# Two attentions over 257 keys: maxima by bank, one product for the last keys of four batches, heads added ahead of the output projection

## The chip, the cores and the metric

One core of one Trainium2 chip runs the whole program. The metric is the device time of one execution in microseconds, the median of several runs. The engines are TensorE (PE in the rows; PEld is its weight load), VectorE (DVE), ScalarE (ACT), GpSimd (POOL) and SyncE (SP, which here issues DMAs). Each engine works through its own list of instructions in order, and they meet at semaphores.

## The reference

A perceiver of four layers on x (128 batches, 32 tokens, 128 features) with a context of 257 keys for each batch. Each layer has a cross-attention, a self-attention (or a scan) and a feed-forward part. The change lies in the cross-attentions of layers 1 and 2. Cut to what matters (the norms of q and k in layer 1 and the mask of layer 2 are left out; 16 heads of 8 features):

```
q = x1 @ Wq.T ; k = ctx @ Wk.T ; v = ctx @ Wv.T      # split into 16 heads
s = einsum('bhqd,bhkd->bhqk', q, k) * scale          # 32 x 257 for each batch and head
a = softmax(s, axis=-1)
o = einsum('bhqk,bhkd->bhqd', a, v)                  # heads side by side: 32 x 128
x = x + o @ Wo.T + bo
```

## The kernel before

`cross_attention` is called twice: in stage l1x_att (keys already projected and stored in KA, fetched by DMA into kT) and in stage l2x_att (KA is None: the keys are projected here, and there is a mask). It handles one batch at a time. The 16 heads are four groups j of four: the group j lies on partitions 32j to 32j + 31, and within it each of the 128 rows of the score product is one (head of four, query) pair. So a batch has four score products of 128 x 257, one in each of the four banks of pS. In float32 a product is issued as two passes, so the rows show x8 for four products, x4 for two.

The keys 0 to 255 and the last key 256 are handled apart. For the first 256: maxima over pS (`maxima`, DVE, L2666: two reduces, of two banks each), exponentials with their sums (`exponentials`, ACT, L2626, one for each bank, into prob), reciprocals (`factors`, DVE, L2671), scaling (`scale`, POOL, L2427), eight turns of 128 x 128 (`turn`, PE, L2546, into the banks pT), copies of them (`keep_turned`: half by DVE, L2688, half by ACT, L2633, into probT), and `attend` (PE, L2559), which gives O: feature by (head of four, query). `own_head` (DVE, L2698 or L2695) multiplies O with the mask m4, so that for each feature only its own head of the four is left, and stores it in own[:, h, b, :], b being the batch's place in a group of four. `output` (PE, L2566) then runs once for four batches: X = sum over h of own[:, h] @ wo, four products, and to the same X it adds the last keys' part.

The last key: its probabilities of four batches are gathered in tail (POOL, L2433) and turned on PE (`turn_tails`, L2508) to 16 rows (batch, j); `keep_tails` (DVE, L2681) multiplies them with batch16 into pbd, so that a row counts for its own batch alone. Its values, masked by head (vm, POOL, L2438), are multiplied with wo in four products (`last_keys`, PE, L2514, two in each of two slots), which ACT copies to mt (L2618). `output` multiplies pbd with mt, four products with 16 rows (L2570), into X. DVE adds X to the residual (`add`, L2704); POOL adds the bias bo.

The order is written by hand. `run_slots4` calls `slot(n, c, k)` on each engine, with c = n % 4 and k = n // 4: in slot n, PE makes the scores of batch n + 1, attends for n - 2, turns n - 1 and makes the values of n + 2 (and in l2x_att its keys, ahead of the turns). Work that belongs to four batches stands in slots chosen by c. The slots with 4 <= n < 124 are a loop over four slots; below, a slot is named by its c. The bank pKV holds in turn the keys' projection (columns 0 to 256), the values (0 to 255), and at its end the last keys' products and the turned tails (columns 256 to 511), so `bank_read` and `bank_free` make PE wait until it has been read: in l2x_att for k_kept, DVE's copy kT (L2676). `after(eng, sem, n)` waits until unit n is through; s_made is counted twice for each batch.

In this excerpt of PE's slot, the lines that the order turns on:

```python
if c == 0 and inside(n - 4):
    turn_tails(k - 1)
...
if c == 0 and inside(n - 4):
    pe.wait_ge(pb_made, made(k - 1))
...
if c == 3 and inside(n):
    last_keys(k, 0)
if c == 0 and inside(n - 4):
    last_keys(k - 1, 1)
...
if c == 1 and inside(n - 5):
    output(k - 1)
```

`cosine_attention` (stage l3a_att) is another function; its POOL instruction at L1867 waits for s_made as well.

## Time and profile before

| | us |
|---|---|
| median of 3 runs | 4020.48 |
| lowest, highest | 4013.39, 4028.0 |
| span of the profiled execution | 4018.7 |

The page gives the profiled execution's span (from the first to the last instruction) and no time of its own beside it.

| engine | busy, whole span | busy, l1x_att 900 to 1300 us | busy, l2x_att 1980 to 2420 us |
|---|---|---|---|
| PE | 3136.4 (78%) | 361.96 of 400 | 420.93 of 440 |
| DVE | 2425.2 (60%) | 251.13 | 289.26 |
| ACT | 2065.1 (51%) | 287.05 | 284.75 |
| POOL | 1963.5 (49%) | 251.94 | 246.82 |

The scores of l1x_att begin at 827.0 us and its last operations are at 1342.7; those of l2x_att at 1905.4 and 2482.1. An execution is read from the profile like this: a timeline row gives the start, how long a run of like instructions took, the engine, the line, what is written and read, and in brackets how long the engine had sat idle and who ended that. The start of the same line's next run gives the slot.

### The profile page before, as it was taken

The numbers are of one execution on the slowest core, as the hardware profiler recorded it, in microseconds if no ns is written. First come the engines' busy times: TensorE is split into PE (matmuls) and PEld (weight loads), VectorE is DVE, ScalarE is ACT, GpSimd is POOL, SyncE is SP. The second block draws the span as 40 slices with busy tenths as digits, with TensorE's granted clock in tenths as the row PEclk, the third lists the DMA queues.
The fourth block names the chain that finished last, engine by engine and source line by source line (L and its number), as shares of the span: only waits on it lengthen the run. The fifth ranks groups of instructions, "written<-read, shape, count | busy, mean of one in ns | idle before, by whom it ended". The sixth has DMA issues, their size and how long they took to land. (4 is left out here: it accounts for less than half of the span.)

```text
span 4018.7 us, 81101 instructions
## 1 busy us (share of the span) xinstructions
PE 3136.4 (78%) x24323; PEld 2160.5 (54%) x24323; DVE 2425.2 (60%) x5893; ACT 2065.1 (51%) x6409; POOL 1963.5 (49%) x1960
## 2 busy tenths in 40 slices
...
DMA packets 138613, 233.70 MB, mean 58 GB/s; under 512 B 28428, under 2 KB 100398, under 8 KB 137623
## 3 DMA queue, kind: packets, MB, share of 16 engines
...
q8 instruction: 103, 1.69, 0.2%
...
## 5 line engine op out<-in xcount | busy, mean ns | idle before, releaser
L2427 POOL TENSOR_TENSOR l2x_att_prob<-l2x_att_prob,l2x_att_rs 128x1024 f32<-128x1024 f32 x128 | 242.2, 1893 | 253.2 <-DVE l2x_att_rs L2671 253.2
L3200 PE MATMUL l2a_pY<-l2a_hc,ident 128*128 128x512 f32 x512 | 275.0, 677 | 90.3 <-POOL l2a_hc L3119 56.1
L2427 POOL TENSOR_TENSOR l1x_att_prob<-l1x_att_prob,l1x_att_rs 128x1024 f32<-128x1024 f32 x128 | 242.2, 1893 | 190.6 <-DVE l1x_att_rs L2671 190.6
L2626 ACT ACTIVATE l2x_att_prob<-l2x_att_pS,l2x_att_nmx 128x257 f32<-128x257 f32 x512 | 236.2, 474 | 169.4 <-DVE l2x_att_nmx L2666 169.4
L3089 POOL TENSOR_TENSOR l2a_dbu<-l2a_dx,l2a_BC 128x1024 f32<-128x1024 f32 x128 | 298.5, 2352 | 21.5 <-PE l2a_pY L3200 10.7
L2626 ACT ACTIVATE l1x_att_prob<-l1x_att_pS,l1x_att_nmx 128x257 f32<-128x257 f32 x512 | 236.2, 474 | 129.7 <-DVE l1x_att_nmx L2666 129.7
L3217 ACT ACTIVATE l2a_pA<-l2a_dl,l2a_A 128x512 f32<-128x512 f32 x256 | 174.4, 689 | 188.8 <-DVE l2a_pH L3323 113.0
L3200 PEld LDWEIGHTS l2a_pY<-l2a_hc,ident 128*128 128x128 f32 x512 | 103.7, 211 | 253.2 <-issue 120.0
L3323 DVE TENSOR_TENSOR_SCAN l2a_pH<-l2a_pA,l2a_dbu 128x512 f32<-128x512 f32 x192 | 224.8, 1216 | 23.6 <-POOL l2a_dbu L3089 12.2
L2666 DVE TENSOR_REDUCE l2x_att_nmx<-l2x_att_pS 128x2 f32<-128x514 f32 x256 | 165.5, 688 | 115.7 <-PE l2x_att_pS L2534 113.0
L2666 DVE TENSOR_REDUCE l1x_att_nmx<-l1x_att_pS 128x2 f32<-128x514 f32 x256 | 165.5, 689 | 92.4 <-PE l1x_att_pS L2527 92.3
L1963 ACT ACTIVATE l3a_att_prob<-l3a_att_pS,l3a_att_nmx 128x128 f32<-128x128 f32 x512 | 179.6, 397 | 8.2 <-DVE l3a_att_nmx L2000 4.1
L1874 POOL TENSOR_TENSOR l3a_att_prob<-l3a_att_prob,l3a_att_rs 128x512 f32<-128x512 f32 x128 | 130.4, 1041 | 56.7 <-DVE l3a_att_rs L2021 56.7
L2207 POOL TENSOR_SCALAR l1x_KA<-l1x_k_y,l1x_k_cols 128x257 f32<-128x257 f32 x128 | 118.0, 940 | 53.3 <-DVE l1x_k_y L2329 53.3
L2546 PE MATMUL l1x_att_pT<-ident,l1x_att_prob 128*128 128x128 f32 x1024 | 139.0, 279 | 0.0
L2546 PE MATMUL l2x_att_pT<-ident,l2x_att_prob 128*128 128x128 f32 x1024 | 133.7, 274 | 0.0
L2546 PEld LDWEIGHTS l2x_att_pT<-ident,l2x_att_prob 128*128 128x128 f32 x1024 | 119.5, 142 | 14.2 <-issue 0.6
L2546 PEld LDWEIGHTS l1x_att_pT<-ident,l1x_att_prob 128*128 128x128 f32 x1024 | 112.0, 142 | 19.5 <-issue 13.4
...
L3330 DVE TENSOR_TENSOR l2a_hc<-l2a_pH,l2a_BC 128x512 f32<-128x512 f32 x192 | 121.7, 676 | 0.0
L1963 ACT ACTIVATION_READ_ACCUMULATOR l3a_att_prob<-l3a_att_pS,l3a_att_nmx 128x1 f32 x512 | 120.9, 236 | 0.0
L2527 PE MATMUL l1x_att_pS<-l1x_att_kT,l1x_att_qb 32*128 32x257 f32 x1024 | 96.5, 432 | 19.5 <-ACT l1x_att_prob L2626 17.6
...
## 6 DMA issues: line engine op xcount, KB each, us to landing
l2a_BC<-l2a_rows SPq DMA_DIRECT2D x128, 512.0 KB, 3.8
...
l1x_att_ctx<-ctx_t SPq DMA_DIRECT2D x128, 128.5 KB, 2.1
l1x_att_kT<-l1x_KA SPq DMA_DIRECT2D x128, 128.5 KB, 2.2
l2x_att_ctx<-ctx_t SPq DMA_DIRECT2D x128, 128.5 KB, 2.1
...
```

The costliest lines, as they stand in the source:

```text
L1874: pool.tensor_tensor(x, x, bc(rs[:, n % 2, R * j:R * j + R], 2, P), ALU.mult).then_inc(scaled, 1)
L1963: last = act.activation(prob[:, n % 3, h, :], pS[:, j, h % R * P:(h % R + 1) * P], ACT.Exp, bias=nmx[:, n % 2, h:h + 1], accum_out=sums[:, ...
L2207: pool.tensor_scalar(parts[i].dst[:, piece(n, u)], y[:, n % 3, u, 0:width(n)], cols[i][:, 0:1], None, ALU.add).then_inc(done, 1)
L2427: pool.tensor_tensor(p, p, bc(rs[:, b, :], 2, LAST), ALU.mult).then_inc(scaled, 1)
L2546: last = pe.transpose(pT[h][:, j * P:(j + 1) * P], prob[:, b, j, h * P:(h + 1) * P], env.ident[:, :])
L2626: last = act.activation(prob[:, b, j, 0:KEYS], pS[:, j, 0:KEYS], ACT.Exp, bias=nmx[:, b, j:j + 1], accum_out=sums[:, b, j:j + 1])
L2666: dve.tensor_reduce(nmx[:, b, 2 * u:2 * u + 2], pS[:, 2 * u:2 * u + 2, 0:KEYS], AX.X, ALU.max, negate=True).then_inc(m_made, 1)
L3089: pool.tensor_tensor(dbu[:, u % 3], dx[:, g % 2], bc(BC[:, u % RING, 0, :], 1, NC), ALU.mult).then_inc(dbu_made, 1)
L3200: last = pe.matmul(pY[c][:, :], env.ident[:, :], hc[:, u % 3, c, :], start=False, stop=n == NS - 1)
L3217: act.activation(pA[c][:, :], dl[:, g % 2, c, :], ACT.Exp, scale=A[:, c, n:n + 1]).then_inc(da_made, 1)
L3323: dve.tensor_tensor_scan(h, pA[c][:, :], dbu[:, u % 3, c, :], 0.0, ALU.mult, ALU.add).then_inc(h_made, 1)
L3330: dve.tensor_tensor(hc[:, u % 3, c, :], pH[c][:, :], BC[:, u % RING, 1, :], ALU.mult).then_inc(hc_dve, 1)
```

## The change

- *Maxima.* All four score products of a batch give one signal, s_made (one count for each batch; the waits on it in `queries`, SP's loads and `keys` are rewritten to that). DVE makes four reduces of 128 x 257, each with its own signal, and each exponential waits for its own bank's. PE waits for p_made once for each batch as before.
- *Last keys.* tail, vm, pbd and mt have 128 rows: row 32 h + (batch, j), 16 of 32 used in each quarter; vm and tail are cleared once by two memsets on POOL. `last_keys` is one product of 128 x 128 in c = 0 (L2520 of the new file), copied by one ACT instruction of 128 x 128. `turn_tails` is four products of 32 x 32 into the bank of O and X (the tile PT), in c = 1 behind `attend`. `keep_tails` is one instruction of 128 x 128, in c = 1 too. batch32 is loaded in place of batch16. `output` has one product for the last keys in place of four.
- *Heads.* A new DVE reduce, `sum_heads` (c = 1), adds own over h into osum (128 x 128, four elements each, 128 elements apart); `output` has one product with wo in place of four, and waits for osum_made. On DVE, pbd and the sum stand between `own_head` and, in l2x_att, `keys` (kT), and ahead of `keep_turned`. `own_head` waits for pt_made in the fourth batch of a group, and for osum_made in the first.
- *Others.* POOL adds the bias behind `queries`. In `cosine_attention`, POOL's wait ahead of kb is `n - 2` for `2 * (n - 2) + 1`, s_made being counted twice a batch there still; the names of the stages are unchanged.

The diff, cut to its core:

```diff
@@ cosine_attention, gpsimd
-                    after(pool, s_made, 2 * (n - 2) + 1)
+                    after(pool, s_made, n - 2)
@@ cross_attention
-        m16, batch16 = st.sb("m16", [P, R, R]), st.sb("batch16", [16, BT])
-        vm, tail = st.sb("vm", [P, R, 16]), st.sb("tail", [P, BT, R])
-        pbd, mt = st.sb("pbd", [16, R, BT, S]), st.sb("mt", [16, R, D])
+        m16, batch32 = st.sb("m16", [P, R, R]), st.sb("batch32", [P, BT])
+        vm, tail = st.sb("vm", [P, R, 32]), st.sb("tail", [P, 32])
+        pbd, mt = st.sb("pbd", [P, BT, S]), st.sb("mt", [P, D])
+        osum = st.sb("osum", [P, BT, S])
...
-        O, X = pO[:, 0:P], pO[:, P:2 * P]
+        O, X, PT = pO[:, 0:P], pO[:, P:2 * P], pO[:, 2 * P:2 * P + S]
+        M = pKV[:, 3 * D:4 * D]
@@ gpsimd
+                pool.memset(vm[:, :, :], 0.0).then_inc(cleared, 1)
+                pool.memset(tail[:, :], 0.0).then_inc(cleared, 1)
...
@@ tensor
-                def turn_tails(k):
-                    pe.wait_ge(tail_kept, made(2 * k + 1))
-                    pe.wait_ge(mo_kept, made(2 * k))
-                    pe.transpose(pKV[0:16, 3 * D:4 * D], tail[:, :, :].rearrange("p b j -> p (b j)"), env.ident[:, :]
-                                 ).then_inc(pt_made, 1)
+                def turn_tails():
+                    for h in range(R):
+                        r = slice(32 * h, 32 * h + 32)
+                        last = pe.matmul(PT[r, :], tail[r, :], env.ident[r, r])
+                    last.then_inc(pt_made, 1)
...
+                def last_keys(k):
                     pe.wait_ge(vm_made, made(k))
+                    after(pe, mo_kept, k - 1)
+                    pe.matmul(M, vm[:, :, :].rearrange("p h j -> p (h j)"), wo[:, :]).then_inc(mo_made, 1)
...
                 def output(g):
-                    pe.wait_ge(own_made, made(4 * g + 3))
-                    for h in range(R):
-                        pe.matmul(X, own[:, h].rearrange("p b q -> p (b q)"), wo[:, :], start=h == 0, stop=False)
-                    pe.wait_ge(mo_kept, made(2 * g + 1))
+                    pe.wait_ge(osum_made, made(g))
+                    pe.matmul(X, osum[:, :, :].rearrange("p b q -> p (b q)"), wo[:, :], start=True, stop=False)
+                    pe.wait_ge(mo_kept, made(g))
                     pe.wait_ge(pb_made, made(g))
-                    for h in range(R):
-                        last = pe.matmul(X, pbd[:, h].rearrange("p b q -> p (b q)"), mt[:, h, :], start=False,
-                                         stop=h == R - 1)
-                    last.then_inc(out_made, 1)
+                    pe.matmul(X, pbd[:, :, :].rearrange("p b q -> p (b q)"), mt[:, :], start=False, stop=True
+                              ).then_inc(out_made, 1)
...
+                    if c == 1 and inside(n - 5):
+                        pe.wait_ge(tail_kept, made(2 * (k - 1) + 1))
                     if inside(n - 2):
                         attend(n - 2, (c - 2) % 4, k if c >= 2 else k - 1)
+                    if c == 1 and inside(n - 5):
+                        turn_tails()
@@ scalar
-                def exponentials(n, b, k, u):
-                    act.wait_ge(m_made, made(2 * n + u))
+                def exponentials(n, b, k):
...
-                    for j in (2 * u, 2 * u + 1):
+                    for j in range(R):
+                        act.wait_ge(m_made, made(R * n + j))
@@ vector
-                def maxima(n, b, u):
-                    dve.wait_ge(s_made, made(2 * n + u))
-                    dve.tensor_reduce(nmx[:, b, 2 * u:2 * u + 2], pS[:, 2 * u:2 * u + 2, 0:KEYS], AX.X, ALU.max,
-                                      negate=True).then_inc(m_made, 1)
+                def maxima(n, b):
+                    dve.wait_ge(s_made, made(n))
+                    for j in range(R):
+                        dve.tensor_reduce(nmx[:, b, j:j + 1], pS[:, j, 0:KEYS], AX.X, ALU.max, negate=True
+                                          ).then_inc(m_made, 1)
...
+                def sum_heads(k):
+                    dve.wait_ge(own_made, made(4 * k + 3))
+                    after(dve, out_made, k - 1)
+                    dve.tensor_reduce(osum[:, :, :].rearrange("p b q -> p (b q)"),
+                                      own[:, :, :, :].rearrange("p h b q -> p (b q) h"), AX.X, ALU.add
+                                      ).then_inc(osum_made, 1)
```

PE in the loop of l1x_att, slot c = 0 (pS are the scores, pO attend's products, pT the turns, pKV here the last keys' products and, from L2502 or L2508 of the new file, the values; REGISTER_ALU and ISA rows belong to waits). Before:

```order
L2527 MATMUL l1x_att_pS<-l1x_att_kT,l1x_att_qb 128x257 x4
L1449 REGISTER_ALU
L2559 MATMUL l1x_att_pO<-l1x_att_probT,l1x_att_v 32x128 x8
L2506 ISA
L2507 REGISTER_ALU
L2508 MATMUL l1x_att_pKV<-ident,l1x_att_tail 16x128
L2541 REGISTER_ALU
L2546 MATMUL l1x_att_pT<-ident,l1x_att_prob 128x128 x8
L2587 REGISTER_ALU
L2497 REGISTER_ALU
L2514 MATMUL l1x_att_pKV<-l1x_att_wo,l1x_att_vm 16x128 x2
L2502 MATMUL l1x_att_pKV<-l1x_att_wv,l1x_att_ctx 128x128 x2
```

and after:

```order
L2532 MATMUL l1x_att_pS<-l1x_att_kT,l1x_att_qb 128x257 x4
L2553 REGISTER_ALU
L1449 REGISTER_ALU
L2561 MATMUL l1x_att_pO<-l1x_att_probT,l1x_att_v 32x128 x8
L2543 REGISTER_ALU
L2548 MATMUL l1x_att_pT<-ident,l1x_att_prob 128x128 x8
L2503 REGISTER_ALU
L2518 REGISTER_ALU
L2520 MATMUL l1x_att_pKV<-l1x_att_wo,l1x_att_vm 128x128
L2508 MATMUL l1x_att_pKV<-l1x_att_wv,l1x_att_ctx 128x128 x2
```

The turned tails left this slot, and one product of 128 x 128 stands where two of 16 rows stood.

PE in the same loop, slot c = 1. Before:

```order
L2527 MATMUL l1x_att_pS<-l1x_att_kT,l1x_att_qb 128x257 x4
L2559 MATMUL l1x_att_pO<-l1x_att_probT,l1x_att_v 32x128 x8
L2541 REGISTER_ALU
L2546 MATMUL l1x_att_pT<-ident,l1x_att_prob 128x128 x8
L2502 MATMUL l1x_att_pKV<-l1x_att_wv,l1x_att_ctx 128x128 x2
L2566 MATMUL l1x_att_pO<-l1x_att_wo,l1x_att_own 128x128 x4
L2570 MATMUL l1x_att_pO<-l1x_att_mt,l1x_att_pbd 128x128 x4
```

and after:

```order
L2532 MATMUL l1x_att_pS<-l1x_att_kT,l1x_att_qb 128x257 x4
L2577 ISA
L2561 MATMUL l1x_att_pO<-l1x_att_probT,l1x_att_v 32x128 x8
L2514 MATMUL l1x_att_pO<-ident,l1x_att_tail 32x32 x4
L2548 MATMUL l1x_att_pT<-ident,l1x_att_prob 128x128 x8
L2508 MATMUL l1x_att_pKV<-l1x_att_wv,l1x_att_ctx 128x128 x2
L2567 MATMUL l1x_att_pO<-l1x_att_wo,l1x_att_osum 128x128
L2570 MATMUL l1x_att_pO<-l1x_att_mt,l1x_att_pbd 128x128
```

The tails are turned here, behind attend; the output is two products for eight.

DVE in the loop of l2x_att, slot c = 1 (rs reciprocals, nmx maxima, own the masked copy, kT the keys' copy, probT the copy of the turns, pbd the last keys' probabilities, osum the sum over heads). Before:

```order
L2671 RECIPROCAL l2x_att_rs<-l2x_att_sums 128x4
L2665 ISA
L2666 TENSOR_REDUCE l2x_att_nmx<-l2x_att_pS 128x2
L2665 REGISTER_ALU
L2666 TENSOR_REDUCE l2x_att_nmx<-l2x_att_pS 128x2
L2695 SCALAR_TENSOR_TENSOR l2x_att_own<-l2x_att_pO,l2x_att_cols,m 128x4x32
L2674 REGISTER_ALU
L2676 TENSOR_SCALAR l2x_att_kT<-l2x_att_pKV,l2x_att_cols 128x257
L2686 REGISTER_ALU
L2688 COPY l2x_att_probT<-l2x_att_pT 128x512
```

and after:

```order
L2665 RECIPROCAL l2x_att_rs<-l2x_att_sums 128x4
L2660 TENSOR_REDUCE l2x_att_nmx<-l2x_att_pS 128x1 x4
L2692 REGISTER_ALU
L2694 REGISTER_ALU
L2699 SCALAR_TENSOR_TENSOR l2x_att_own<-l2x_att_pO,l2x_att_cols,m 128x4x32
L1449 REGISTER_ALU
L2676 TENSOR_TENSOR l2x_att_pbd<-l2x_att_pO,l2x_att_batch 128x128
L2682 TENSOR_REDUCE l2x_att_osum<-l2x_att_own 128x128
L2668 REGISTER_ALU
L2670 TENSOR_SCALAR l2x_att_kT<-l2x_att_pKV,l2x_att_cols 128x257
L2687 ISA
L2689 COPY l2x_att_probT<-l2x_att_pT 128x512
```

Two instructions came between own and kT, and the two reduces of the maxima are four.

## Rows read from the trace of the kernel before

**Rows 1.** Windows: from:to, length, busy us by engine, PEclk (granted clock), DMA share, GB/s

```profile
526.00:608.00 82.00, 62.64 (x155) 24.14 (x155) 72.35 (x298) 3.04 (x6) 1.69 (x2) 0.94 0.02 4
900.00:1300.00 400.00, 361.96 (x4269) 270.38 (x4271) 251.13 (x556) 287.05 (x1060) 251.94 (x303) 1.00 0.23 66
1980.00:2420.00 440.00, 420.93 (x4781) 314.63 (x4779) 289.26 (x643) 284.75 (x1041) 246.82 (x296) 1.00 0.12 30
```

**Rows 2.** Timeline of l1x_att: start us, took us, engine line, names, count [idle before]

```profile
1001.50 0.72 PE L2527 MATMUL l1x_att_pS<-l1x_att_kT,l1x_att_qb 32*128 32x257 f32 x8 [0.44 <-ACT l1x_att_prob L2626]
...
1002.25 1.29 DVE L2666 TENSOR_REDUCE l1x_att_nmx<-l1x_att_pS 128x2 f32<-128x514 f32 x2 [0.59 <-PE l1x_att_pS L2527]
...
1003.07 0.48 ACT L2626 ACTIVATE l1x_att_prob<-l1x_att_pS,l1x_att_nmx 128x257 f32<-128x257 f32 x1 [0.86 <-DVE l1x_att_nmx L2666]
...
1003.66 0.68 DVE L2688 COPY l1x_att_probT<-l1x_att_pT 128x512 f32<-128x512 f32 x1
...
1003.74 0.61 PE L2514 MATMUL l1x_att_pKV<-l1x_att_wo,l1x_att_vm 128*16 128x128 f32 x4
...
1004.79 0.21 ACT L2626 ACTIVATION_READ_ACCUMULATOR l1x_att_prob<-l1x_att_pS,l1x_att_nmx 128x1 f32 x1
...
1005.06 0.72 PE L2527 MATMUL l1x_att_pS<-l1x_att_kT,l1x_att_qb 32*128 32x257 f32 x8
...
1009.39 0.72 PE L2527 MATMUL l1x_att_pS<-l1x_att_kT,l1x_att_qb 32*128 32x257 f32 x8
...
1013.75 0.49 PE L2527 MATMUL l1x_att_pS<-l1x_att_kT,l1x_att_qb 32*128 32x257 f32 x3
...
1017.34 0.72 PE L2527 MATMUL l1x_att_pS<-l1x_att_kT,l1x_att_qb 32*128 32x257 f32 x8 [0.44 <-ACT l1x_att_prob L2626]
```

**Rows 3.** Timeline of l2x_att, one group of four slots

```profile
2203.23 0.49 PE L2527 MATMUL l2x_att_pS<-l2x_att_kT,l2x_att_qb 32*128 32x257 f32 x3
...
2206.91 0.72 PE L2527 MATMUL l2x_att_pS<-l2x_att_kT,l2x_att_qb 32*128 32x257 f32 x8
...
2209.84 0.60 PE L2514 MATMUL l2x_att_pKV<-l2x_att_wo,l2x_att_vm 128*16 128x128 f32 x4
...
2210.38 0.71 PE L2502 MATMUL l2x_att_pKV<-l2x_att_wv,l2x_att_ctx 128*128 128x128 f32 x4
...
2211.02 0.71 PE L2527 MATMUL l2x_att_pS<-l2x_att_kT,l2x_att_qb 32*128 32x257 f32 x8
...
2215.84 0.72 PE L2527 MATMUL l2x_att_pS<-l2x_att_kT,l2x_att_qb 32*128 32x257 f32 x8
...
2216.69 1.29 DVE L2666 TENSOR_REDUCE l2x_att_nmx<-l2x_att_pS 128x2 f32<-128x514 f32 x2 [1.58 <-PE l2x_att_pS L2534]
...
2218.16 0.48 DVE L2676 TENSOR_SCALAR l2x_att_kT<-l2x_att_pKV,l2x_att_cols 128x257 f32<-128x257 f32 x1
...
2218.69 0.71 PE L2502 MATMUL l2x_att_pKV<-l2x_att_wv,l2x_att_ctx 128*128 128x128 f32 x4
...
2219.24 1.06 PE L2566 MATMUL l2x_att_pO<-l2x_att_wo,l2x_att_own 128*128 128x128 f32 x8
...
2220.22 1.04 PE L2570 MATMUL l2x_att_pO<-l2x_att_mt,l2x_att_pbd 16*128 16x128 f32 x7
...
2221.00 0.49 PE L2527 MATMUL l2x_att_pS<-l2x_att_kT,l2x_att_qb 32*128 32x257 f32 x3
```

**Rows 4.** Groups by line, DVE: form xcount | busy us, mean ns | idle before

```profile
L2666 DVE TENSOR_REDUCE l1x_att_nmx<-l1x_att_pS 128x2 f32<-128x514 f32 x256 | 165.5, 689 | 92.4 <-PE l1x_att_pS L2527 92.3
...
L1761 DVE TENSOR_REDUCE l1a_att_sums<-l1a_att_prob 128x16 f32<-128x512 f32 x32 | 21.8, 680 | 2.3 <-ACT l1a_att_prob L1688 2.1
...
L3656 DVE TENSOR_REDUCE l3x_att_m<-l3x_att_pS 128x1 f32<-128x257 f32 x32 | 13.6, 425 | 14.4 <-PE l3x_att_pS L3541 14.4
...
L814 DVE TENSOR_TENSOR l1f_list_z<-l1f_list_pp,l1f_list_cum 128x256 f32<-128x256 f32 x1 | 0.6, 585 | 0.0
...
L812 DVE TENSOR_TENSOR l1f_list_cum<-l1f_list_cum,l1f_list_tot 128x256 f32<-128x256 f32 x1 | 0.4, 425 | 0.0
```

More of the change, by code:

```diff
@@ L2415, in _ @@
                 st.open(pool)
+                pool.memset(vm[:, :, :], 0.0).then_inc(cleared, 1)
+                pool.memset(tail[:, :], 0.0).then_inc(cleared, 1)
                 pool.wait_ge(loaded, 16 * len(loads))
                 pool.wait_ge(vt_kept, 1)
+                pool.wait_ge(cleared, 2)
                 def queries(n, b):
-                    after(pool, s_made, 2 * (n - 2) + 1)
+                    after(pool, s_made, n - 2)
                     pool.tensor_tensor(qb[:, b % 2], bc(QT[:, bass.ds(n * S, S)], 1, R), bc(env.m4[:, :], 2, S),
@@ L2451, in slot @@
                         queries(n + 2, c + 2)
+                    if c == 0 and inside(n):
+                        x = env.X[:, k, :]
+                        pool.tensor_tensor(x, x, bo[:, :], ALU.add).then_inc(biased, 1)
                     if c == 1 and inside(n):
@@ L2464, in slot @@
                     if KA is not None:
-                        after(sp, s_made, 2 * (n - 2) + 1)
+                        after(sp, s_made, n - 2)
                     sp.dma_start(ctx[:, c % 2, 0:KEYS], env.a.ctx_t[:, bass.ds(n * KEYS, KEYS)]
@@ L2484, in bank_read @@
                     after(pe, v_kept, n - 1)
-                    if c < 2:
-                        after(pe, mo_kept, 2 * (k - 1) + c)
+                    if c == 1:
+                        after(pe, mo_kept, k - 1)
                 def keys(n, c, k):
@@ L2523, in scores @@
                         pe.wait_ge(k_landed[b], landed_count(c, k, 1))
-                    after(pe, p_made, 2 * (n - 1) + 1)
+                    after(pe, p_made, n - 1)
                     for j in range(R):
@@ L2528, in scores @@
                                          start=True, stop=not masked)
-                        if not masked and j % 2:
-                            last.then_inc(s_made, 1)
                     if masked:
@@ L2535, in scores @@
                                              start=False, stop=True)
-                            if j % 2:
-                                last.then_inc(s_made, 1)
+                    last.then_inc(s_made, 1)
                 def turn(n, b, h):
@@ L2636, in slot @@
                     if inside(n + 1):
-                        for u in range(2):
-                            exponentials(n + 1, (c + 1) % 4, k if c < 3 else k + 1, u)
+                        exponentials(n + 1, (c + 1) % 4, k if c < 3 else k + 1)
                     if inside(n - 1):
@@ L2674, in keys @@
                     dve.wait_ge(k_made, made(n))
-                    after(dve, s_made, 2 * (n - 2) + 1)
+                    after(dve, s_made, n - 2)
                     dve.tensor_scalar(kT[:, c % 2, 0:KEYS], pKV[:, 0:KEYS], cols[:, 0:1], None, ALU.add
```

68 lines of the change are left out of this document (28 added, 40 removed).

## The prediction

> **What bounds the kernel now.** I looked first at the windows view [rows 1], then at two timelines, and last at the DVE durations. The two attention stages with 257 keys (l1x_att, some 516 us; l2x_att, some 577 us) keep TensorE busy for 362 of 400 us and 421 of 440 us, with the full clock granted (1.00) [rows 1]. The share alone doesn't say that PE's work is the bound; what repeats, slot after slot, is a ring of waits. In the timeline of l1x_att [rows 2] the reader is to follow one slot (one batch): the scores start at 1001.50; the first of two maxima 0.75 later; the first exponential 0.82 after that; the last read of its sums ends at 1005.00, 1.93 after the first exponential began; and 0.06 later the next scores start at 1005.06. That is 3.56 us, and the PE row at 1001.50 says that it waited for ACT. All four score products end together, so nothing else stands between. Two of four slots are longer: from 1005.06 to 1009.39 (4.33; c = 0, turned tails and the last keys' products) and to 1013.75 (4.36; c = 1, the output products). Four slots take 15.84 us (1001.50 to 1017.34).
> In l2x_att [rows 3] four slots take 17.77 us (2203.23 to 2221.00): 3.68 (c = 2), 4.11 (c = 3), 4.82 (c = 0), 5.16 (c = 1). Here a second ring runs through DVE: scores at 2215.84, maxima 0.85 later, kT at 2218.16 (1.47 after the maxima began) for 0.48, and 0.05 later the values products, which need the bank that kT was read from; 0.64 after values come the next scores (2210.38 to 2211.02).
>
> **The change part by part.** All of it is priced per group of four slots; each stage has 32 groups, and I count 31, since the last drains without new scores.
>
> *Maxima bank by bank.* A reduce of 128x257 from PSUM takes 425 ns in l3x_att, against 689 for the 514 wide one [rows 4]. So the first exponential comes 0.26 us earlier. Nothing is lost by waiting for all four score products. A reduce is issued some 0.08 before its predecessor ends (two of 0.689 take 1.29 in [rows 2]), so four take 4 x 0.425 - 3 x 0.085 = 1.44, which is 0.15 more on DVE. The exponentials start 0.455 apart, further than the 0.34 of the reduces, so only the first waits. Where the ring over ACT decides, a slot goes from 3.56 to 3.30. I take 3.29 (3.55 less 0.26) for c = 2, 3 and 0 of l1x_att. Can PE follow? In c = 3 the scores are followed after 2.24 by the last-key products (1003.74), these after 0.54 by values, these after 0.64 by scores [rows 2, 3]: 3.42, with them. Now they are gone from c = 3, and in c = 0 one product (two passes) stands for four passes: 2.24 + 0.32 + 0.64 = 3.20, just under 3.29. So c = 0 falls from 4.33 to 3.29; the turned tails, and PE's wait for pbd, leave that slot.
> In l2x_att the DVE ring takes over: 0.85 + (1.47 + 0.15) + 0.48 + 0.05 puts values at 3.00 and the next scores at 3.64. The ACT ring would give 3.42. So c = 2 goes from 3.68 to 3.64, c = 3 from 4.11 to 3.64, and c = 0, with one product more (0.32), from 4.82 to 3.96.
>
> *Last keys as one 128-row product.* Two passes for eight, one ACT copy of 128x128 for two of 16x256; pbd is 128x128 for 16x512. The pass costs 0.11 (eight from 2219.24 to 2220.22 [rows 3]), and four with their gap take 0.54, so two take 0.32. That is in the slots above. ACT has room: in [rows 2] it idles in each slot before the first exponential. The four 32x32 products that turn the tails stand in c = 1 behind the attend products; between 0.1 and 0.4 us, and hidden in both stages, because PE will wait there for DVE anyway. That cover is some 0.5 us in l1x_att.
> A rule of the Trainium skill speaks against them: "TensorEngine Tiling (Array Packing)", Key Properties, has a change of tiling mode drain the engine. No row prices a change to 32x32; if it were the 0.2 that other gaps show, twice a group, the cover above would still hold it.
>
> *Heads added on DVE.* The output falls from 16 passes (2219.24 to 2221.00: 1.76) to four: 0.32 + 0.42 = 0.74, the 0.42 being two passes and the 0.20 that values show ahead of scores (0.64 - 0.44). It now waits for the sum of 512 elements, which stands behind four maxima, the masked copy and pbd. A contiguous reduce of 512 takes 680 ns [rows 4]. But this one reads each element 512 bytes from the last. The nearest row is L814: a tensor_tensor whose SBUF input steps by 128 bytes takes 585 ns, where L812 of the same 256 elements takes 425 [rows 4]: 0.625 ns more for each. For 512 elements that is 0.32, so I take 1.00 us, and keep 0.68 as the lower end; the upper end is open, and I put it at 1.3.
> The Trainium skill has the same: "SBUF — State Buffer", Specifications (TRN2), says of cachelines that one needs two hits per line for full bandwidth and that "each cross to a new line pays a penalty". By that rule L814's extra is the line crossing, and the trace agrees (585 against 425); without it the sum would be 20 us lower.
> In l1x_att, c = 1: the copy of probT starts 1.41 after the first maximum [rows 2]; that place, 0.15 later, is now pbd's: 0.75 + 1.56 = 2.31. Then pbd (0.20 on the queue), the sum (1.00) and 0.05: PE goes on at 3.56, and the next scores start at 3.56 + 0.74 = 4.30. Before it was 4.36, so the slot gains almost nothing: 12 passes are paid for with a wait.
> In l2x_att, c = 1, kT is queued behind pbd and the sum: values at 3.00 + 0.20 + 0.92 = 4.12, output 0.55 later (2218.69 to 2219.24), scores 0.74 after that: 5.41. Before 5.16: this slot is longer. Queued behind the sum there are also the copy of probT and the reciprocal; both have over 0.5 us left, since PE's next scores are late too.
>
> *Free edits.* The waits of POOL and SP on s_made count one per batch for two: the same event. POOL's x + bias goes behind the queries; POOL is busy for 252 of 400 us [rows 1], so it isn't late. The two memsets run once in a stage, while loads land. The edited wait in cosine attention (l3a) is met in both forms, as POOL has waited for rs_made of the same batch: no effect.
>
> **The sum.** l1x_att: 3 x 3.29 + 4.30 = 14.17 for 15.84, saves 1.67. l2x_att: 3.64 + 3.64 + 3.96 + 5.41 = 16.65 for 17.77, saves 1.12. Together 2.79 x 31 = 86.5. The profiled execution's span is 4018.7; less 86.5 it is 3932.2. The median of the runs shown is 1.8 above that span, so I predict 3934.
>
> **Rivals.**
> *A, the strided sum costs no more than a contiguous one (0.68):* 0.32 x 62 less: 3914. For it: the other input of L814, from PSUM, steps too, and no reduce in the trace has such a step. Against it: the 160 ns.
> *B, the maxima help less.* If the reduces don't overlap, each slot of l2x_att and c = 1 of l1x_att get 0.26 more: 5 x 0.26 x 31 = 40, so 3974. If the exponentials gain nothing from the earlier first maximum, 3 x 0.26 x 31 = 24, so 3958. Against both: the pair in [rows 2] overlaps, and ACT's row names the maxima.
> *C, slower: the strided sum becomes the bound.* Each microsecond of it beyond 1.00 costs 62 us, as PE (and kT) wait for it once a group. From 2.4 us on the change loses; at four times the contiguous price (2.7) the time is 3934 + 105 = 4039. Against it: it needs 4.7 ns an element where L814 shows 1.7 at most.
> *D, the change doesn't do what it says:* the passes taken from PE are not where PE is waited for, and the slots stay as they are: some 4015. The waits for ACT in [rows 2] speak for it, the 4.33 and 4.82 of c = 0 against it.
> *E, PE's clock falls,* since PE is busy for less. I give it no chance of its own: l1x_att is busy for 14.3 of 15.84 us (362 of 400); if as much as 3.3 us of it went, 11.0 of 14.17 (78%) would be left, and a stretch with 62.6 of 82 us (76%) has 0.94 [rows 1].
>
> **How the numbers follow.** Forecast 3934: 0.47. A (3914): 0.22. B (3958 to 3974): 0.16. D: 0.05. C: 0.05. Still faster than 3900 (the output's gaps shorter): 0.05. The range takes in A with short gaps and all of B: 3900 to 3975. A measurement of this kernel tells 0.3% (12 us) from no change: faster 0.89, same 0.05, slower 0.06.
>
> **What would show it.** Scores 3.29 apart in three of four slots of l1x_att; a reduce of 257 at 425 ns; the sum at 1.00 us, with PE idle behind it in c = 1; in l2x_att values waiting for kT in every slot. Wrong would be: a sum at 0.7 or far over 1; c = 0 in l1x_att above 3.5 (then PE, not ACT, bounds it); attend products waiting for turned tails.

## The result, and the profile after the change

The changed kernel takes 3913.98 us (median of 4 runs, 3907.33 to 3936.55), where the kernel before, run beside it, takes 4020.24: a ratio of 0.9743 (95% interval 0.9712 to 0.9774). Timed again later, in one set with two other kernels, it has 0.9775 (0.9751 to 0.9799). The profiled execution's span is 3908.6 us, 110.1 less than the 4018.7 of before.

The windows view of the changed kernel (columns as in [rows 1]; the busy times are those of PE, PEld, DVE, ACT and POOL), l1x_att, l2x_att, and l0f_exp, a stage ahead of both:

```profile
900.00:1240.00 340.00, 292.44 (x3795) 219.66 (x3796) 263.52 (x746) 264.05 (x988) 240.15 (x288) 1.00 0.26 74
1900.00:2340.00 440.00, 399.95 (x4822) 293.15 (x4822) 330.17 (x928) 301.23 (x1086) 264.98 (x318) 1.00 0.12 32
460.00:589.00 129.00, 98.77 (x320) 46.07 (x320) 97.30 (x388) 13.84 (x30) 6.82 (x8) 0.88 0.02 5
```

In both stages PE's share falls (86% for 90%, 91% for 96%), and the clock stays at 1.00.

Timeline of l1x_att after the change, where [rows 2] stood before; the slots c = 0 (1006.64 to 1009.97) and c = 1 (to 1014.22):

```profile
1006.64 0.72 PE L2532 MATMUL l1x_att_pS<-l1x_att_kT,l1x_att_qb 32*128 32x257 f32 x8 [0.46 <-ACT l1x_att_prob L2622]
...
1008.79 0.39 PE L2520 MATMUL l1x_att_pKV<-l1x_att_wo,l1x_att_vm 128*128 128x128 f32 x2
...
1009.97 0.72 PE L2532 MATMUL l1x_att_pS<-l1x_att_kT,l1x_att_qb 32*128 32x257 f32 x8 [0.34 <-ACT l1x_att_prob L2622]
...
1010.74 1.42 DVE L2660 TENSOR_REDUCE l1x_att_nmx<-l1x_att_pS 128x1 f32<-128x257 f32 x4 [0.71 <-PE l1x_att_pS L2532]
...
1011.19 0.26 PE L2514 MATMUL l1x_att_pO<-ident,l1x_att_tail 32*32 32x32 f32 x8
...
1011.38 1.09 PE L2548 MATMUL l1x_att_pT<-ident,l1x_att_prob 128*128 128x128 f32 x8
...
1012.28 0.28 DVE L2676 TENSOR_TENSOR l1x_att_pbd<-l1x_att_pO,l1x_att_batch 128x128 f32<-128x128 f32 x1
...
1012.48 1.05 DVE L2682 TENSOR_REDUCE l1x_att_osum<-l1x_att_own 128x128 f32<-128x512 f32 x1
...
1013.58 0.49 PE L2567 MATMUL l1x_att_pO<-l1x_att_wo,l1x_att_osum 128*128 128x128 f32 x2 [0.66 <-DVE l1x_att_osum L2682]
1013.90 0.39 PE L2570 MATMUL l1x_att_pO<-l1x_att_mt,l1x_att_pbd 128*128 128x128 f32 x2
...
1014.22 0.72 PE L2532 MATMUL l1x_att_pS<-l1x_att_kT,l1x_att_qb 32*128 32x257 f32 x8
```

c = 0 takes 3.33 us and its scores still wait for ACT, so it has joined the short slots. In c = 1 PE stands idle for 0.66 us behind the sum of the heads, and the four output passes fill the 0.64 from 1013.58 to 1014.22.

The same slot c = 1 of l2x_att, in place of the one from 2215.84 to 2221.00 in [rows 3]:

```profile
2111.71 0.72 PE L2532 MATMUL l2x_att_pS<-l2x_att_kT,l2x_att_qb 32*128 32x257 f32 x8
...
2112.58 1.42 DVE L2660 TENSOR_REDUCE l2x_att_nmx<-l2x_att_pS 128x1 f32<-128x257 f32 x4 [1.26 <-PE l2x_att_pS L2537]
...
2114.37 1.05 DVE L2682 TENSOR_REDUCE l2x_att_osum<-l2x_att_own 128x128 f32<-128x512 f32 x1
...
2115.33 0.48 DVE L2670 TENSOR_SCALAR l2x_att_kT<-l2x_att_pKV,l2x_att_cols 128x257 f32<-128x257 f32 x1
...
2115.87 0.71 PE L2508 MATMUL l2x_att_pKV<-l2x_att_wv,l2x_att_ctx 128*128 128x128 f32 x4 [1.06 <-DVE l2x_att_kT L2670]
2116.41 0.39 PE L2567 MATMUL l2x_att_pO<-l2x_att_wo,l2x_att_osum 128*128 128x128 f32 x2
...
2116.95 0.72 PE L2532 MATMUL l2x_att_pS<-l2x_att_kT,l2x_att_qb 32*128 32x257 f32 x8
```

The sum stands ahead of kT on DVE, values wait 1.06 us for kT, and the slot takes 5.24 us where it took 5.16. The groups by line of the new DVE work (columns as in [rows 4]):

```profile
L2660 DVE TENSOR_REDUCE l1x_att_nmx<-l1x_att_pS 128x1 f32<-128x257 f32 x512 | 182.0, 418 | 85.7 <-PE l1x_att_pS L2532 85.7
...
L2682 DVE TENSOR_REDUCE l1x_att_osum<-l1x_att_own 128x128 f32<-128x512 f32 x32 | 33.6, 1050 | 0.0
```

All slots of a group, in us from scores to scores (medians over the loop of each stage), as predicted and as the traces have them. "Stages" is the length of l1x_att and l2x_att from first to last use, added:

| | l1x c=2 | c=3 | c=0 | c=1 | group | l2x c=2 | c=3 | c=0 | c=1 | group | stages |
|---|---|---|---|---|---|---|---|---|---|---|---|
| before | 3.58 | 3.56 | 4.34 | 4.36 | 15.83 | 3.68 | 4.10 | 4.82 | 5.16 | 17.77 | 1110.4 |
| predicted | 3.29 | 3.29 | 3.29 | 4.30 | 14.17 | 3.64 | 3.64 | 3.96 | 5.41 | 16.65 | |
| after | 3.33 | 3.22 | 3.33 | 4.26 | 14.13 | 3.64 | 3.72 | 4.02 | 5.25 | 16.62 | 1020.0 |
| e2 | 3.31 | 3.43 | 4.47 | 4.36 | 15.57 | 3.74 | 4.23 | 4.92 | 5.29 | 18.18 | 1114.5 |
| e3 | 3.32 | 3.22 | 3.33 | 4.02 | 13.89 | 3.64 | 3.72 | 4.02 | 4.95 | 16.33 | 1004.1 |
| e4 | 3.32 | 3.22 | 3.32 | 3.91 | 13.78 | 3.64 | 3.72 | 4.02 | 4.91 | 16.30 | 997.6 |
| e5 | 3.59 | 3.49 | 3.59 | 4.13 | 14.80 | 3.68 | 3.58 | 3.89 | 5.12 | 16.27 | 1031.5 |
| e7 | 3.72 | 3.23 | 3.33 | 3.32 | 13.60 | 3.73 | 3.67 | 4.02 | 3.84 | 15.25 | 962.5 |
| e8 | 3.63 | 3.23 | 3.57 | 3.32 | 13.76 | 3.80 | 3.68 | 3.74 | 3.86 | 15.08 | 960.2 |
| e10 | 3.59 | 3.49 | 3.59 | 4.00 | 14.68 | 3.68 | 3.59 | 3.89 | 4.82 | 15.97 | 1018.2 |
| e11 | 3.31 | 3.22 | 3.32 | 3.31 | 13.17 | 3.80 | 3.68 | 3.73 | 3.85 | 15.06 | 942.1 |

The stages lose 90.4 us, against 86.5 forecast. The span lost 110.1. The missing 20 us are the first question. The lengths of the stages carry 1 to 2 us of their own: a second trace of the kernel before (e1) has 1108.9 for 1110.4, one of the changed kernel (e9) 1020.4 for 1020.0.

### The profile page after: what moved, and what is told of

Same layout as the page of the kernel before. It is cut to its first block and busy times, and to the rows that moved or that the text cites. A ratio compares the mean times of both kernels' runs of the same rounds, so it can differ in the third digit from the quotient of the medians.

```text
span 3908.6 us, 79627 instructions
## 1 busy us (share of the span) xinstructions
PE 2978.2 (76%) x23619; PEld 2035.7 (52%) x23619; DVE 2481.4 (63%) x6469; ACT 2048.3 (52%) x6345; POOL 1967.2 (50%) x1964
## 5 line engine op out<-in xcount | busy, mean ns | idle before, releaser
L2660 DVE TENSOR_REDUCE l2x_att_nmx<-l2x_att_pS 128x1 f32<-128x257 f32 x512 | 182.0, 418 | 110.3 <-PE l2x_att_pS L2537 110.3
L2660 DVE TENSOR_REDUCE l1x_att_nmx<-l1x_att_pS 128x1 f32<-128x257 f32 x512 | 182.0, 418 | 85.7 <-PE l1x_att_pS L2532 85.7
```

What stands on the lines that cost most here:

```text
L2660: dve.tensor_reduce(nmx[:, b, j:j + 1], pS[:, j, 0:KEYS], AX.X, ALU.max, negate=True).then_inc(m_made, 1)
```

## Experiments

Each ratio is that of the run's median to the median of the kernel before, timed in the same set: 4016.76 us for e2 to e4, 4004.27 for e5 to e8, 4027.84 for e9 to e11. Where two edited kernels are compared, it is by their stages and slots.

**e1: the kernel before once more.**

> The kernel before once more, not edited, for its trace. The two attention stages with 257 keys got shorter by 52.7 us (522.7 to 470.0) and 37.7 us (587.7 to 550.0), together 90.4; the span by 110.1. The rest, some 20 us, lies in stages that the change doesn't touch, most of it ahead of them: l0f_exp went from 140.1 to 128.2 us, l0f_logits from 32.0 to 25.7. Theory: that part is chance, as the clock that TensorE gets in these stages falls out one way or the other in each execution, so here l0f_exp may come out at either length, and the sum of all stages but the two may differ from that of the first trace by 10 us or more. Rival: the change causes it (other constants, other addresses of the program), so l0f_exp takes 140 again and all stages but the two agree with the first trace within 3 us.

It took 4008.89 us (one run). The two stages are where they were (522.5 and 586.4), but l0f_exp takes 128.2 us, l0f_logits 25.6. The windows of l0f_exp in the first trace of before, and in this second one of the same program:

```profile
458.00:598.00 140.00, 111.22 (x320) 54.52 (x320) 97.28 (x388) 13.95 (x30) 6.80 (x8) 0.80 0.02 4
```
```profile
458.00:586.00 128.00, 98.74 (x320) 46.05 (x320) 95.87 (x382) 13.84 (x30) 6.80 (x8) 0.89 0.01 4
```

The same 320 passes take 111.2 or 98.7 us, at a mean granted clock of 0.80 or 0.89. In all thirteen traces of this study, l0f_exp has one of these two lengths (128.1 to 128.2 in five, 140.0 to 140.3 in eight), and either kernel has had both. So 18 us of the 110 (l0f_exp and l0f_logits) are chance, and the rival falls. The other stages aren't fixed either: this trace has the 18 us less than the first, and its span is only 11.6 us shorter (4007.1 for 4018.7). What decides between the two lengths stays open.

**e2: maxima bank by bank, alone.**

```diff
-  dve.tensor_reduce(nmx[:, b, 2*u:2*u+2], pS[:, 2*u:2*u+2, 0:KEYS], AX.X, ALU.max, negate=True).then_inc(m_made, 1)
+  for j in (2*u, 2*u+1):
+      dve.tensor_reduce(nmx[:, b, j:j+1], pS[:, j, 0:KEYS], AX.X, ALU.max, negate=True).then_inc(m_made, 1)
```

> The kernel before with the maxima taken bank by bank (four reduces, each exponential waiting for its own), and nothing else. Theory: the edit is worth something only where the ring over ACT sets the slot, and it puts 0.15 us more ahead of what is queued behind it on DVE. l1x_att: c = 2 from 3.58 to 3.32, c = 3 from 3.56 to 3.42 (then PE with its last-key passes), c = 0 from 4.34 to 4.49 (PE waits for pbd, which is 0.15 later), c = 1 4.36 as before: 0.25 saved for each group. l2x_att: kT is 0.15 later in each slot: c = 2 3.64 for 3.68, c = 3 4.18 for 4.10, c = 0 4.97 for 4.82, c = 1 5.30 for 5.16: 0.33 lost for each group. Together 31 x 0.08 = 2 us more: the time stays, 4023. Rival: the edit is worth its 0.26 in every slot, whatever else is there: 8 x 0.26 x 31 = 64 us less, 3956.

4020.74 us, a ratio of 1.0017 (0.9996 to 1.0038): no gain. In l1x_att the slots moved as the theory had them: c = 2 loses 0.27, c = 0 grows by 0.13. In l2x_att every slot grows, c = 2 as well, where the theory had a small gain (3.74, not 3.64). Timeline of e2, l2x_att, c = 0 (scores at 2108.58), with what stands ahead of pbd on DVE:

```profile
2109.43 1.42 DVE L2667 TENSOR_REDUCE l2x_att_nmx<-l2x_att_pS 128x1 f32<-128x257 f32 x4 [1.48 <-PE l2x_att_pS L2534]
...
2111.42 0.67 DVE L2682 TENSOR_TENSOR l2x_att_pbd<-l2x_att_pKV,l2x_att_batch 16x512 f32<-16x512 f32 x1
```
```profile
2112.32 0.60 PE L2514 MATMUL l2x_att_pKV<-l2x_att_wo,l2x_att_vm 128*16 128x128 f32 x4 [0.73 <-DVE l2x_att_pbd L2682]
```

Four reduces take 1.42 for the 1.29 of two, and what waits behind them on DVE waits that much longer.

**e3: the heads summed by PE again.**

```diff
-  pe.wait_ge(osum_made, made(g))
-  pe.matmul(X, osum[:, :, :].rearrange("p b q -> p (b q)"), wo[:, :], start=True, stop=False)
+  pe.wait_ge(own_made, made(4 * g + 3))
+  pe.wait_ge(pb_made, made(g))
+  for h in range(R):
+      pe.matmul(X, own[:, h].rearrange("p b q -> p (b q)"), wo[:, :], start=h == 0, stop=False)
...
```

(with `sum_heads` gone from DVE, and `own_head` waiting for the output in its place).

> The changed kernel without the sum of the heads on DVE: four products of own with wo (8 passes) stand again in the output, the rest as changed. Theory: the sum of 1.05 us holds up more than the six passes that it spares. l1x_att, c = 1: values at 2.34, output at 2.79, ten passes 1.3 to 1.35, so 4.1 for 4.25. l2x_att, c = 1: kT 1.0 earlier, values at 3.25, output at 3.8, so 5.1 for 5.25. The other slots don't move. 0.3 x 31 = 9 us less than the changed kernel: 3905. Rival, PE's work is what counts: six passes of 0.11 more in two stages, 0.66 x 62 = 41 us more: 3955.

3895.49 us, ratio 0.9686 (0.9663 to 0.9709). Only c = 1 moved: 0.24 shorter in l1x_att, 0.30 in l2x_att, and the stages 15.9 us shorter. Timeline of e3, l2x_att, c = 1 (scores at 2105.05):

```profile
2108.24 0.71 PE L2508 MATMUL l2x_att_pKV<-l2x_att_wv,l2x_att_ctx 128*128 128x128 f32 x4
2108.79 1.06 PE L2569 MATMUL l2x_att_pO<-l2x_att_wo,l2x_att_own 128*128 128x128 f32 x8
2109.69 0.39 PE L2572 MATMUL l2x_att_pO<-l2x_att_mt,l2x_att_pbd 128*128 128x128 f32 x2
2110.00 0.72 PE L2532 MATMUL l2x_att_pS<-l2x_att_kT,l2x_att_qb 32*128 32x257 f32 x8
```

Eight passes of own run from 2108.79 to 2109.69, 0.90 us; two take 0.23 (2116.41 to 2116.64 in the changed kernel), so the sum spares 0.67 of PE's time. It costs 0.96 in DVE's queue (the next instruction starts that much after the sum does). This third part of the change is a loss of 16 us.

**e4: own with the heads innermost.**

```diff
-  own = st.sb("own", [P, R, BT, S])
+  own = st.sb("own", [P, BT, S, R])
```

(with the accesses to it in keeping).

> The changed kernel with own laid out so that the four heads of an element lie side by side: the sum reads 512 contiguous elements, and the masked copy that fills own writes with a step of 16 bytes. Theory, the price of the sum is its step: it falls from 1.05 to 0.68, which takes 0.37 off c = 1 of both stages, 0.37 x 62 = 23 us; the masked copy (0.28 and 0.34) gets dearer by 0 to 0.15, which only l2x_att feels, 0 to 0.6 x 31 = 0 to 19 us: 3891 to 3910. Rival, the price is that of 128 short groups of four and not of the step: the sum stays at 1.05, and the time is 3914 to 3933.

3897.49 us, ratio 0.9704 (0.9677 to 0.9730); stages 22.4 us shorter. Groups by line of e4:

```profile
L2699 DVE SCALAR_TENSOR_TENSOR l2x_att_own<-l2x_att_pO,l2x_att_cols,m 128x128 f32<-128x128 f32 x128 | 57.8, 452 | 3.7 <-PE l2x_att_pO L2561 2.2 <-PE l2x_att_pO L2514 1.5
...
L2682 DVE TENSOR_REDUCE l1x_att_osum<-l1x_att_own 128x128 f32<-128x512 f32 x32 | 21.8, 681 | 0.0
```

The sum falls from 1050 to 681 ns, the price of a contiguous one in [rows 4]: 0.37 us for 512 elements, 0.72 ns each, where L814 gave me 0.625. The masked copy grows from 343 to 452 ns in the record, but kT starts only 0.02 later behind it (279 ns after the copy's start for 258, medians over the stage), and kT's own record is 15 ns shorter, so that the other slots of l2x_att stay as they were. A timeline piece of e4 (2106.18 to 2106.47, 0.29; one of the changed kernel has 0.25):

```profile
2106.18 0.45 DVE L2699 SCALAR_TENSOR_TENSOR l2x_att_own<-l2x_att_pO,l2x_att_cols,m 128x128 f32<-128x128 f32 x1
2106.47 0.46 DVE L2670 TENSOR_SCALAR l2x_att_kT<-l2x_att_pKV,l2x_att_cols 128x257 f32<-128x257 f32 x1
```

The step costs on the reading side of the sum and next to nothing on the writing side of the copies. The rule that the prediction cites from the Trainium skill ("SBUF — State Buffer", Specifications (TRN2)), that each new line costs, agrees with the sum: 1050 against 681. It doesn't show in what follows the copies, 0.02. No run here tells the crossing of lines from another price of a step of 512 bytes.

**e5: maxima in pairs again, the rest as changed** (e2's edit, taken back).

> The changed kernel with the maxima as before (two reduces of two banks each, the first exponential of a pair waits for it), the rest as changed. Theory: the reduces bank by bank gain in l1x_att, where the ring over ACT sets the slot, and lose in l2x_att, where they stand ahead of kT on DVE. l1x_att: c = 2 and c = 0 from 3.32 to 3.58, c = 3 from 3.22 to 3.48, c = 1 (the sum 0.15 earlier) from 4.25 to 4.10: 0.63 longer for each group. l2x_att: kT 0.13 earlier, but the ring over ACT then stands at 3.68: c = 2 3.68 for 3.64, c = 3 3.68 for 3.72, c = 0 3.88 for 4.02, c = 1 5.11 for 5.25: 0.27 shorter. Together 0.36 x 31 = 11 us more: 3925. Rival, each slot gets its 0.26 back: 8 x 0.26 x 31 = 64 us more, 3978.

3929.48 us, ratio 0.9794 (0.9750 to 0.9837). In the stages: l1x_att 21.2 us longer, l2x_att 9.7 shorter, 11.5 us in all. So this edit is worth 11 us in the company of the other two parts, and nothing alone (e2).

**e6: the sum made twice.**

```diff
+  dve.tensor_reduce(osum_2[:, :], own[:, :, :, :].rearrange("p h b q -> p (b q) h"), AX.X, ALU.add)
```

> The changed kernel with the sum of the heads made twice (the first into a tile that nobody reads). Theory, PE and kT wait for the sum once in a group: c = 1 gets 0.96 longer in both stages (1.05 less the 0.09 by which one starts ahead of its predecessor's end), 5.21 in l1x_att and 6.20 in l2x_att, no other slot changes, 0.96 x 62 = 60 us more than the changed kernel, 3974. Rival, something else is as late as the sum, so that only part of it arrives, or the delay spreads to the slot behind it and costs more.

4005.41 us (one run, with the long form of l0f_exp); the stages are 77.9 us longer, not 60. The median of c = 1 is as expected (5.21 and 6.20). But in 8 of the 31 groups of l1x_att the slot behind it takes 4.1 to 4.4 us for 3.33, and in 7 of those of l2x_att some 4.86 for 3.64. Timeline and windows of e6 around one of them:

```profile
949.48 0.49 PE L2567 MATMUL l1x_att_pO<-l1x_att_wo,l1x_att_osum 128*128 128x128 f32 x2 [1.61 <-DVE l1x_att_osum L2683]
...
950.12 0.72 PE L2532 MATMUL l1x_att_pS<-l1x_att_kT,l1x_att_qb 32*128 32x257 f32 x8
...
951.52 1.97 PE L2548 MATMUL l1x_att_pT<-ident,l1x_att_prob 128*128 128x128 f32 x8
```
```profile
943.40:950.10 6.70, 4.75 (x59) 3.72 (x57) 5.78 (x15) 5.00 (x19) 3.60 (x6) 1.00 0.27 79
950.10:954.30 4.20, 4.19 (x41) 3.27 (x40) 2.75 (x9) 2.54 (x9) 3.14 (x4) 0.64 0.22 63
```

Eight transposes take 1.97 us for 1.09: behind a PE idle time of 1.61 us the granted clock is 0.64, so for most of the slot it stood at the lower level of 1.2 GHz. That is rival E, which the prediction had judged by PE's busy share of a whole group; here the fall stands behind one idle time in it, of 1.61 us in l1x_att and 2.01 in l2x_att. In the changed kernel, with 0.66 and 1.06 idle, the clock stays at 1.00 in every slot of the loop.

**e7: the sum in DVE's idle time.** The sum goes behind the reciprocal of c = 2, the output products into c = 2 behind the transposes, X + output into c = 3.

```diff
   if c == 1 and inside(n - 5):
       keep_tails(k - 1)
-      sum_heads(k - 1)
...
   if c == 2 and inside(n - 6):
-      add(k - 1)
+      sum_heads(k - 1)
+  if c == 3 and inside(n - 7):
+      add(k - 1)
...
```

(that is DVE's part; PE's `output` moves from c = 1 to c = 2, behind a new wait for the masked copy of own.)

> The changed kernel with the sum of the heads moved from c = 1, ahead of kT and of the copy of probT, to c = 2 right behind the reciprocal, where DVE stands idle for 0.7 (l1x_att) to 0.9 us (l2x_att) until the scores are there; the output products stand in c = 2 behind the transposes, X + output in c = 3. The work is the same. Theory, what the changed kernel loses in c = 1 is a place in the queue: l1x_att c = 1 from 4.25 to 3.32, c = 2 from 3.32 to 3.6 (the sum outlasts the gap by 0.3), 0.65 shorter; l2x_att c = 1 from 5.25 to 3.85, c = 2 from 3.64 to 4.0 (PE's four passes), 1.04 shorter. 1.69 x 31 = 52 us less: 3862. Rival, DVE's or PE's load is what counts and not the place: then the time that leaves c = 1 comes back in c = 2, and it stays at 3914.

3866.17 us, ratio 0.9643 (0.9608 to 0.9677); stages 57.5 us shorter than in the changed kernel, with the same work on each engine. Timeline of e7, l1x_att, the start of c = 2 and the output in it:

```profile
1006.68 0.18 DVE L2667 RECIPROCAL l1x_att_rs<-l1x_att_sums 128x4 f32<-128x4 f32 x1
1006.78 1.07 DVE L2684 TENSOR_REDUCE l1x_att_osum<-l1x_att_own 128x128 f32<-128x512 f32 x1
1006.80 0.71 PE L2532 MATMUL l1x_att_pS<-l1x_att_kT,l1x_att_qb 32*128 32x257 f32 x8 [0.36 <-ACT l1x_att_prob L2624]
...
1007.76 1.41 DVE L2662 TENSOR_REDUCE l1x_att_nmx<-l1x_att_pS 128x1 f32<-128x257 f32 x4
...
1009.43 0.49 PE L2567 MATMUL l1x_att_pO<-l1x_att_wo,l1x_att_osum 128*128 128x128 f32 x2 [0.32 <-DVE l1x_att_own L2704]
```

The sum fills the time until the scores are there and only 0.2 more: the maxima start 0.96 after the scores for 0.78 in the changed kernel. In c = 2 of l1x_att PE also waits 0.32 for own, and the slot takes 3.72 for the 3.6 expected. The rival, that load and not place counts, falls. The 57.5 us aren't the place of the sum alone, since the four passes of the output left c = 1 with it; no run moves the one without the other.

**e8: e7 with e4's layout, and the last keys' product in the bank of the output.**

```diff
-  M = pKV[:, 3 * D:4 * D]
+  M = pO[:, 3 * P:4 * P]
```

(with `last_keys` behind the transposes and a wait for the masked copy of own, and the attend products of c = 1 waiting for the copy of M).

> The kernel of e7, with own laid out so that the heads lie side by side (as in e4), and with the last keys' product written to the bank of the output and not to that of keys and values, so that it needn't wait for kT: it stands behind the transposes in c = 0. Theory: the sum of 0.68 fits in DVE's gap, so c = 2 of l1x_att falls from 3.6 to 3.42 (PE's own work); c = 0 of l2x_att falls from 4.02 to 3.72. l1x_att 13.28, l2x_att 15.32 for a group, 67 us less than the changed kernel: 3847. Rival: the new waits on the shared bank (the attend products of c = 1 wait for ACT's copy of the last keys' product) cost what they save; then e7 and this one are within 10 us.

3857.41 us, ratio 0.9614 (0.9580 to 0.9649). l2x_att is 6.8 us shorter than in e7, l1x_att 4.5 longer. The rival's number came true: the medians of e7 and e8 are 8.8 us apart, the stages 2.3, and 3857 is 10 above the forecast. Sharing the bank makes PE wait for own in c = 0 of l1x_att, where it gets there first (0.42; that slot takes 3.57 for 3.33). The wait in c = 2 (0.23) e7 had already. Timeline of e8:

```profile
1002.61 0.46 PE L2518 MATMUL l1x_att_pO<-l1x_att_wo,l1x_att_vm 128*128 128x128 f32 x2 [0.42 <-DVE l1x_att_own L2702]
...
1009.31 0.49 PE L2567 MATMUL l1x_att_pO<-l1x_att_wo,l1x_att_osum 128*128 128x128 f32 x2 [0.23 <-DVE l1x_att_own L2702]
```

**e9, e10, e11**, timed in one set; before has a median of 4027.84 us in it. In all three l1f_exp takes 150.4 to 152.6 us, where the ten other traces have 129.9 to 132.3, so their times are compared with each other alone. The kernel before wasn't traced in this set, so whether its l1f_exp is longer too isn't known, and why it is longer stays open.

**e9: the changed kernel again.**

> The changed kernel once more, not edited, timed in the same rounds as the two others of this set. Theory: 31 x (1.70 + 1.15) = 88 us of the gain over the kernel before is the two stages', and what lies above that in the first comparison (106) is chance, so the gain here is 88 to 95 us; l1x_att 470 and l2x_att 550 us. Rival: the change gains some 105 us each time, and 15 of it outside of these stages.

3942.92 us. The ratio of 0.9775 (0.9751 to 0.9799) is a gain of 91 us (81 to 100); the two medians are 85 apart. Stages 1020.4. The theory's 88 to 95 lies in the interval and the rival's 105 outside of it, but this doesn't settle it: if l1f_exp is long in the traced kernels alone, some 20 us of the gain are hidden here. What repeats is the stages, 88.5 to 90.4 us shorter in any pair of the two traces of each kernel.

**e10: the last keys' part alone** (e3's and e5's edits together in the changed kernel).

> Of the three parts of the change only the last keys in one 128-row product (with the turned tails of c = 1 and POOL's order): the maxima are two reduces of two banks each, and the output has four products of own with wo and one of pbd with mt. Theory, composed from what undoing each part alone did: l1x_att c = 2 and c = 0 3.59, c = 3 3.49, c = 1 4.02 (PE's own work): 14.69 for a group, 1.14 less than before. l2x_att c = 2 3.68, c = 3 3.58, c = 0 3.89, c = 1 4.83: 15.98, 1.79 less than before. Together 2.93 x 31 = 91 us less than before, as much as the whole change (88): the last keys carry it, and the other two parts bring nothing together. Rival, the parts add up as the prediction had them, with the maxima worth 0.26 in the three slots of l1x_att that ACT sets and in l2x_att what is left: then it is 20 to 30 us slower than the changed kernel.

3941.59 us, ratio 0.9775 (0.9746 to 0.9803), 1018.2 us in the stages. Neither the time nor the sum of the stages tells it from the changed kernel, though its slots do. The rival falls.

With e3 and e5 the stages now price each part in company. The last keys take 92.2 us off (1110.4 to 1018.2); the maxima, added to them, 14.1 more (e3, 1004.1); the sum of the heads on DVE gives 15.9 back (1020.0), or 13.3 with the maxima in pairs (e5 against this run). That the part alone is as fast as the whole is two effects that cancel.

The 2.95 us that the last keys' part saves in the two groups come from c = 0 (1.68), c = 1 (0.70) and c = 3 (0.58). It is itself an edit of shape and of order, and no run separates the two.

**e11: each stage in its own order.** In l1x_att M stays in pKV and the output products stand behind values; l2x_att as e8.

> e8 with each stage in its own order: in l1x_att the last keys' product stays in the bank of keys and values, and the output products stand behind values, so that PE waits for the masked copy of own in neither place; l2x_att as in e8. Theory: in e8 PE waited in l1x_att 0.42 and 0.23 us for own before products that write its bank; without it c = 0 falls from 3.57 to 3.32 and c = 2 from 3.63 to 3.42. l1x_att 13.3, l2x_att 15.08: 0.46 x 31 = 14 us less than e8, 2.4 x 31 = 73 us less than the changed kernel, so 3841 to 3845. Rival: the masked copy is late for c = 2 in either order, and only c = 0 gains: 3849.

3864.26 us, ratio 0.9580 (0.9557 to 0.9602), 79 us below the changed kernel of the same set (stages 78.3, and 18.1 below e8, where 14 were expected). The time named in the expectation, 3841 to 3845, was missed: it lacked the 20 us of l1f_exp. The difference was to be 73. Timeline of e11, PE in c = 2 of l1x_att:

```profile
1002.18 0.72 PE L2532 MATMUL l1x_att_pS<-l1x_att_kT,l1x_att_qb 32*128 32x257 f32 x8 [0.36 <-ACT l1x_att_prob L2634]
...
1004.33 0.61 PE L2508 MATMUL l1x_att_pKV<-l1x_att_wv,l1x_att_ctx 128*128 128x128 f32 x4
1004.78 0.44 PE L2569 MATMUL l1x_att_pO<-l1x_att_wo,l1x_att_osum 128*128 128x128 f32 x2
1005.05 0.39 PE L2572 MATMUL l1x_att_pO<-l1x_att_mt,l1x_att_pbd 128*128 128x128 f32 x2
1005.50 0.72 PE L2532 MATMUL l1x_att_pS<-l1x_att_kT,l1x_att_qb 32*128 32x257 f32 x8
```

The output follows values without a wait, and the slot is 3.32 us. By its stages it is the fastest version found; its ratio's interval overlaps with that of e8.

## Why the prediction held, step by step

*The two rings.* Right. l1x_att has three slots of 3.22 to 3.33 (forecast 3.29), each with its scores waiting for ACT, and in l2x_att the pass behind kT waits for it in every slot, values in c = 1 to 3 and the last keys' product in c = 0. Timeline of the changed kernel, c = 3 of l2x_att (scores at 2103.97; PEld is the weight load of values):

```profile
2106.96 0.52 PEld L2508 LDWEIGHTS l2x_att_pKV<-l2x_att_wv,l2x_att_ctx 128*128 128x128 f32 x4 [0.33 <-DVE l2x_att_kT L2670]
```

That is 3.00 behind the scores, as forecast. The slot is 0.08 above the forecast all the same: its next scores start 0.72 behind values, not 0.64. I found no cause for that, nor for the 0.1 by which c = 3 of l1x_att is shorter than its neighbours.

*Maxima.* The sizes were right: a reduce of 418 ns (425), four in 1.42 (1.44). What the prediction didn't separate is that the edit gains in one stage and loses in the other, and that it needs the rest of the change to gain anything (e2 against e5).

*Last keys.* Right, and larger than the text made plain: the turned tails leave c = 0, pbd with them, and this part alone gives all of the gain (e10: 92.2 us in the stages, the whole change 90.4). The price of a pass, 0.11, was right too, though the row it was read from gives 0.12 (0.98 for eight): that trace lacks one of the eight records of pbd (x7), and eight passes take 0.90 in e3.

*Turned tails.* Hidden, as said. Eight passes of 32x32 take 0.19 us of PE's time (1011.19 to 1011.38). They start 0.58 behind the start of the attend products (1010.61), as the 128x128 transposes do in c = 3 (1004.07 to 1004.64, 0.57). By the Trainium skill ("TensorEngine Tiling (Array Packing)", Key Properties) a change of tiling mode drains the engine; what of it these eight passes bring is somewhere in the 0.19, and no more than that.

*Heads on DVE.* The sum took 1.05 where I took 1.00 (what stands behind it starts 0.96 later, where I had 0.92), and c = 1 came out at 4.26 and 5.25 for 4.30 and 5.41: the passes needed 0.64 and 0.54, where I had 0.74, since the gap of 0.20 isn't there behind the output products of l2x_att. The gain of 0.20 in these two slots is partly given back in c = 3 and c = 0 of l2x_att (0.14 together), and 31 groups with 1.70 and 1.15 less make 88. The prediction said that this part pays for PE's passes with a wait; it did not weigh the two, and e3 shows that the wait is dearer.

*The median.* Forecast 3934, measured 3914. The stages' term was 3.9 us too small (90.4 for 86.5). The base of the forecast, 4018.7 and 1.8 more, was right: the kernel before took 4020.24 beside the changed one. What the sum has no term for is that stages which the change doesn't touch have two lengths. In the two profiled executions that is 18 us: before had the longer form of l0f_exp, by 12, and of l0f_logits, by 6, the changed kernel the shorter. Which form the other timed runs had isn't on record, so that it also explains the 16 us left between the medians is likely and not shown. The stages, with two traces of each kernel, are the better test of the forecast.

*Rivals.* A gave 3914, the very time measured, and it is false: the stride costs its 0.37 us (e4). B is false (the reduces overlap, the exponentials gain). C's price held in the median slot, 0.95 for 0.96 of a doubled sum, but a delay of that size also brings E, so it would have been dearer than 62 us for each us (77.9 for 0.96). D is false. Two readings of L814 behind A and C were wrong, and neither moved the sum. Its input from PSUM doesn't step: line 814 reads the columns in order, so the one thing said for A wasn't there, but the rise of 160 ns is between an input from PSUM and one from SBUF as well as between steps. And 1.7 ns for each element is L812's (425 for 256); L814 shows 2.3. e4 has the price of the step alone, 0.72 ns.
